# A two-layer Mamba, attention and expert kernel: transposed state sums, convolution on TensorE, wide attention products, and GpSimd's state group scanned in place in SBUF

## What is computed

```python
# layer 0, Mamba
xz = x @ W_in;  x_main, z = split(xz)
x_conv = silu(causal_depthwise_conv(x_main, conv_w, conv_b))     # 4 taps
ssm = x_conv @ W_x                                               # 1 + 16 + 16 columns
delta = softplus(ssm[..., 0:1] * dt_w + dt_b)
A = -exp(A_log)
dA = exp(delta[..., None] * A)
dBx = (delta * x_conv)[..., None] * B_in[:, :, None, :]
# for each time step:  h = dA_t * h + dBx_t ;  y_t = sum over n of h[., n] * C_t[n]
y = (y + D * x_conv) * silu(z)
return y @ W_out
# layer 1, attention, for each of 4 batches and 8 heads
scores = (q + pe) @ (k + pe).T / sqrt(128), causal
attn = softmax(scores) @ v ;  out = attn (all heads side by side) @ Wo.T
```

## Time and profile before

| what | us |
|---|---|
| median of 3 runs (3016.66 to 3021.09) | 3020.17 |
| the profiled execution | 3014.69 |
| its span, first to last instruction | 3013.0 |
| VectorE busy in the span | 2185.5 (73%) |
| TensorE busy in the span | 2631.4 (87%) |
| GpSimd busy in the span | 1233.8 (41%) |
| ScalarE busy in the span | 1230.1 (41%) |

### The profile page before, as it was taken

One profiled execution on the slowest core, in us unless ns is written; L12 is line 12 of the kernel. 1 busy time (PEld: TensorE's weight loads), 2 busy tenths in 40 slices (PEclk: granted clock), 3 DMA queues, 4 the chain that ended last, 5 costly groups with the idle time before them and its releaser, 6 DMA issues. The chain is left out here.

```text
span 3013.0 us, 39940 instructions
## 1 busy us (share of the span) xinstructions
PE 2631.4 (87%) x12440; PEld 1810.1 (60%) x12441; DVE 2185.5 (73%) x4715; ACT 1230.1 (41%) x2272; POOL 1233.8 (41%) x518
## 2 busy tenths in 40 slices
PE   6788888888887759999599999999999999839998
PEld 3233333333433559999377767776777677727776
DVE  4999999999999646666476667766776667525554
ACT  4566566566564215554133324332432243201111
POOL 1698998998999125666000000020002000224444
PEclk8899999999999659999799999999999999959999
DMA  4545555555556253333300000000000000125554
GB/s 154 174 148 179 171 162 172 180 160 178 166 167 189 96 166 59 63 63 58 130 29 1 1 1 29 1 30 16 1 1 29 15 1 1 43 90 127 126 126 72
DMA packets 150095, 269.26 MB, mean 89 GB/s; under 512 B 18300, under 2 KB 106412, under 8 KB 149292
## 3 DMA queue, kind: packets, MB, share of 16 engines
q1 hardware_dynamic: 120972, 227.12, 23.6%
q0 software_dynamic: 28416, 38.05, 7.6%
q10 hardware_dynamic: 544, 2.10, 0.2%
HBM read 209.65 MB, written 57.56 MB: 89 GB/s over the span
## 5 line engine op out<-in xcount | busy, mean ns | idle before, releaser
L692 POOL TENSOR_TENSOR dbx<-u,b_all 128x2048 f32<-128x2048 f32 x128 | 577.6, 4527 | 104.3 <-DVE u L766 49.5
L1677 POOL DMA_INDIRECT slots<-at_r_rows,slot_of x64 | 63.7, 995 | 1171.8 <-DVE slot_of L2022 1153.5
L432 PE MATMUL y_ps<-hc,ident 128*128 128x512 f32 x768 | 403.6, 643 | 117.5 <-DVE hc L846 116.3
L585 ACT ACTIVATE da_ps<-delta,a_neg 128x512 f32<-128x512 f32 x512 | 346.4, 689 | 323.6 <-DVE hc L846 316.7
L1888 ACT COPY at_pt<-at_pt_ps 128x512 f32<-128x512 f32 (+3 forms) x384 | 171.5, 481 | 511.8 <-PE at_pt_ps L1778 510.7
L432 PEld LDWEIGHTS y_ps<-hc,ident 128*128 128x128 f32 x768 | 139.0, 198 | 343.9 <-DVE hc L846 246.5
L1790 PE MATMUL at_o_ps<-at_pt,at_v 128*128 128x128 f32 x2304 | 300.0, 276 | 1.9 <-DVE at_attn L2096 1.9
L1767 PE MATMUL at_s_ps<-at_qk 128*128 128x512 f32 (+3 forms) x768 | 291.4, 489 | 5.0 <-DVE at_v L2072 3.1
L1790 PEld LDWEIGHTS at_o_ps<-at_pt,at_v 128*128 128x128 f32 x2304 | 278.0, 192 | 9.7 <-issue 9.7
L1878 ACT ACTIVATE at_probs<-at_s_ps,at_small 128x128 f32<-128x128 f32 (+7 forms) x256 | 191.8, 749 | 207.9 <-DVE at_small L2083 207.5
L846 DVE TENSOR_TENSOR hc<-da_ps,c_all 128x512 f32<-128x512 f32 x384 | 256.7, 669 | 0.1
(11 more groups left out here) (315 smaller groups left out, 4891.7 us busy)
## 6 DMA issues: line engine op xcount, KB each, us to landing
b_all<-bc_rows SPq DMA_DIRECT2D x128, 512.0 KB, 4.5
c_all<-bc_rows SPq DMA_DIRECT2D x128, 512.0 KB, 4.7
e_w<-L_ffn_w SPq DMA_DIRECT2D x32, 512.0 KB, 5.5
slots<-zeros SPq DMA_DIRECT2D x40, 260.0 KB, 6.3
e_xs<-slots SPq DMA_DIRECT2D x16, 650.0 KB, 7.2
w<-L_ffn_W SPq DMA_DIRECT2D x24, 384.0 KB, 8.9
more<-zeros SPq DMA_DIRECT2D x16, 256.0 KB, 4.5
sums<-x SPq DMA_DIRECT2D x8, 512.0 KB, 7.0
```

The costliest lines, as they stand in the source:

```text
L432: mm = nc.tensor.matmul(y_ps[par][:], sh.ident[:], hc[:, at % RING_H, :], start=False, stop=last)
L585: nc.scalar.activation(da_ps[s % RING_DA][:], delta[:, c % 2, m, :], ACT.Exp, scale=sh.a_neg[:, m, n:n + 1]).then_inc(S["da_ready"], 1)
L692: nc.gpsimd.tensor_tensor(dbx[:, at % RING_DBX], pair, rows, ALU.mult).then_inc(S["dbx_ready"], 1)
```

## The change

Mamba:

- The sum over the states is formed transposed. `sum_states` takes 128x128 slices of `hc` or `own_h` as the stationary side and the identity as the moving one, four PE transposes that accumulate in `y_ps`. After a half, `turn_back` (4 transposes for each channel block) and ScalarE's `take_back` turn y back into `u`.
- For chunks 1 to 7 the convolution leaves VectorE: `convolve` on TensorE adds three matmuls with diagonal tap matrices to the bank, ScalarE's `take_conv` copies the bank to `x_conv`. GpSimd builds the 12 tap matrices at the start (`taps`, in the idle `sh.mods`).
- `delta_product` becomes one matmul that broadcasts row 0 of `bc_sb`; the 128-column copies of w_x go.
- `keep_state` goes to ScalarE, ahead of the decay that takes over the bank.
- The decay of an own step is written to its slot of `own_h` (SBUF), and VectorE's scan reads and writes that slot. The `da_ps` ring then holds other steps alone. ScalarE, no longer VectorE, waits until TensorE has summed the slot's previous content.
- New step numbers in the hand-written order; `gate_y` behind products 8 and 13, `finish_delta` and `multiply_u` both behind product 14 and ahead of product 15.

Attention:

- `weigh` takes half a head (512 query columns) at once: 4 matmuls of 512, 384, 256 and 128 columns, then 8 of 512 (five times), 384, 256 and 128, spread over the following tiles. `keep` copies 128x512, twice per head.
- Two of the eight output tiles are ahead of the last half head's `weigh`.
- `mods2` and its 1 MB load are gone; the rows are loaded per batch into `sh.mods` behind the use of the old ones. `more` shares memory with `attn`; the output of a batch is stored in the loop.

The diff, cut to its core:

```diff
@@ phase_mamba
-        PE_OUT, PE_Z, PE_MAIN, PE_DELTA, PE_BC, PE_NEXT, PE_TURN = (3, 6), (0, 1), (5, 8, 13, 16), 31, 32, (34, 40), (46, 47, 51, 54)
-        ACT_Y, ACT_OUT, ACT_Z, ACT_MAIN, ACT_SILU = 2, (13, 18), (8, 9), (18, 20, 24, 29), 33
-        ACT_RAW, ACT_SOFT, ACT_BC, ACT_NEXT, ACT_XN, ACT_TURN = (36, 38, 41, 44), 46, 42, (52, 53), (51, 53, 55, 59), (62, 63)
-        DVE_OUT, DVE_CONV, DVE_RSTD, ACT_KEEP = (33, 62), (17, 18, 27, 29), 40, 5
-        POOL_W, POOL_GATE, POOL_DELTA, POOL_U, POOL_OWN = 1, 2, 13, 15, 2
+        PE_OUT, PE_Z, PE_MAIN, PE_DELTA, PE_BC, PE_NEXT, PE_TURN = (30, 31), (0, 1), (1, 2, 10, 15), 31, 31, (36, 39), (49, 51, 53, 54)
+        PE_BACK, PE_CONV, ACT_CONV, ACT_BACK = (18, 25, 34, 35), (2, 6, 17, 18), (13, 16, 27, 30), (30, 31, 46, 48)
+        ACT_Y, ACT_OUT, ACT_Z, ACT_MAIN, ACT_SILU = 6, (36, 41), (8, 9), (10, 12, 19, 26), 35
+        ACT_RAW, ACT_SOFT, ACT_BC, ACT_NEXT, ACT_XN, ACT_TURN = (43, 44, 46, 47), 49, 42, (50, 56), (48, 52, 54, 60), (61, 62)
+        DVE_OUT, DVE_RSTD, ACT_KEEP = (36, 41), 36, 6
+        POOL_W, POOL_GATE, POOL_DELTA, POOL_U, POOL_OWN = 6, (8, 13), 14, 14, 2
@@ TensorE
+            def convolve(c, m):
+                pe.wait_ge(S["main_copied"], c * MD + m + 1)
...
+                for j in range(DC - 1):
+                    mm = nc.tensor.matmul(proj_ps[m % 2][:], taps[:, m, j, :], x_main[:, m % 2, j:j + CH], start=False, stop=(j == DC - 2),
+                                          skip_group_check=True)
+                mm.then_inc(S["conv_summed"], 1)
+            def turn_back(c, m):
+                bank_free(c, f"back{m}")
+                pe.wait_ge(S["y_taken"], c * MD + m + 1)
...
+                    mm = nc.tensor.transpose(bank[:, j * P:(j + 1) * P], u[:, c % 2, m, j * P:(j + 1) * P], sh.ident[:])
@@ delta_product
-                    mm = nc.tensor.matmul(proj_ps[1][:], sh.w_delta[:, k, :], x_conv[:, c % 2, k, :],
-                                          start=(k == 0), stop=(k == MD - 1))
+                pe.wait_ge(S["bc_copied"], c + 1)
+                nc.tensor.matmul(proj_ps[1][:], one[:], bc_sb[0:1, :], start=True, stop=True).then_inc(S["delta_done"], 1)
@@ sum_states
-                    mm = nc.tensor.matmul(y_ps[par][:], sh.ident[:], hc[:, at % RING_H, :], start=False, stop=last)
+                for j in range(CT):
+                    at = slice(j * P, (j + 1) * P)
+                    mm = nc.tensor.matmul(y_ps[par][:, at], source[:, at], sh.ident[:], start=False, stop=(last and j == CT - 1), is_transpose=True)
@@ decay (ScalarE)
-                nc.scalar.activation(da_ps[s % RING_DA][:], delta[:, c % 2, m, :], ACT.Exp,
-                                     scale=sh.a_neg[:, m, n:n + 1]).then_inc(S["da_ready"], 1)
+                if is_own(s):
...
+                    elif before >= 0:
+                        act.wait_ge(S["own_summed"], before * GS + i + 1)
+                    out = own_h[:, i // 2, i % 2, :]
+                else:
...
+                    out = da_ps[v % RING_DA][:]
+                    if v >= RING_DA:
+                        act.wait_ge(S["hc_ready"], v - RING_DA + 1)
+                        bc, bs = step_of(v - RING_DA)
+                        if bc % CPB == 0:
+                            nc.scalar.copy(state[:, bs:bs + 1], da_ps[v % RING_DA][:, CH - 1:CH]).then_inc(S["states_kept"], 1)
+                            act.wait_ge(S["states_kept"], hc_at(bc // CPB, bs) + 1)
+                nc.scalar.activation(out, delta[:, c % 2, m, :], ACT.Exp, scale=sh.a_neg[:, m, n:n + 1]).then_inc(S["da_ready"], 1)
@@ scan (VectorE)
-                h = da_ps[s % RING_DA][:]
-                out = h
...
-                    out = own_h[:, i // 2, par, :]
-                nc.vector.tensor_tensor_scan(out, h, dbx[:, at % RING_DBX, i // 2, par, :], 0.0 if c % CPB == 0 else state[:, s:s + 1],
+                h = own_h[:, i // 2, par, :] if is_own(s) else da_ps[hc_at(c, s) % RING_DA][:]
+                nc.vector.tensor_tensor_scan(h, h, dbx[:, at % RING_DBX, i // 2, par, :], 0.0 if c % CPB == 0 else state[:, s:s + 1],
                                              ALU.mult, ALU.add).then_inc(S["scanned"], 1)
@@ phase_attention
-            sp.dma_start(mods2[:], d["mod_rows"][1, 3:5].partition_broadcast(P)).then_inc(S["route_in"], 16)
+            def load_route_mods(rb):
+                sp.wait_ge(S["row_ready"], (rb + 1) * TPB)
...
+                sp.dma_start(sh.mods[:, 0:2, rb, :], d["mod_rows"][1, 3:5, rb].partition_broadcast(P)).then_inc(S["route_in"], 16)
@@ weigh
-                    for j in range(i + 1):
-                        last = nc.tensor.matmul(o_ps[:], v[:, h % 2, j, :], pt[:, n % 2, j, :], start=(j == 0), stop=(j == i))
+                    first = max(j - half * CT, 0) * P
+                    last = nc.tensor.matmul(o_ps[:, first:], v[:, h % 2, j, :], pt[half][:, j, first:], start=(j == 0), stop=(j == (half + 1) * CT - 1))
```

More of the change, by code:

```diff
@@ L160, in phase_mamba @@
         h_in = sb("h_in", [P, 2, KE, CH])
-        bc_sb = sb("bc_sb", [P, CH])
+        bc_sb, one = sb("bc_sb", [1 + 2 * NS, CH]), sb("one", [1, P])
         b_all = sb("b_all", [P, RING_B, 2, CH])
@@ L417, in sum_states @@
                 par = i % 2
-                if k % HS < 2:
-                    halves = c * HALVES + hf
-                    if halves:
-                        pe.wait_ge(S["y_taken"], (halves - 1) * 2 + par + 1)
-                    nc.tensor.matmul(y_ps[par][:], d_diag[:, hf * 2 + par, :], x_conv[:, c % 2, hf * 2 + par, :], start=True, stop=False)
-                last = k % HS >= HS - 2
+                first, last = k % HS < 2, k % HS >= HS - 2
+                halves = c * HALVES + hf
+                if first and halves:
+                    pe.wait_ge(S["y_taken"], (halves - 1) * 2 + par + 1)
+                if first:
+                    for j in range(CT):
+                        at = slice(j * P, (j + 1) * P)
+                        nc.tensor.matmul(y_ps[par][:, at], x_conv[:, c % 2, hf * 2 + par, at], d_diag[:, hf * 2 + par, :], start=(j == 0), stop=False)
                 if g in OWN:
@@ L426, in sum_states @@
                         pe.wait_ge(S["own_ready"], own_to(c, hf, g))
-                    mm = nc.tensor.matmul(y_ps[par][:], sh.ident[:], own_h[:, i // 2, par, :], start=False, stop=last)
-                    mm.then_inc(S["own_summed"], 1)
+                    source, done = own_h[:, i // 2, par, :], S["own_summed"]
                 else:
@@ L673, in _ @@
                 take_y(CHUNKS - 1, m)
+            for m in (2, 3):
+                take_back(CHUNKS - 1, m)
             for pair in range(2):
@@ L729, in _ @@
             nc.gpsimd.memset(sh.zeros[:], 0.0).then_inc(S["zeros_set"], 1)
+            nc.gpsimd.memset(one[:], 1.0).then_inc(S["one_set"], 1)
+            pool.wait_ge(S["ident_set"], 2)
+            pool.wait_ge(small_in, 48)
+            for m in range(MD):
+                for j in range(DC - 1):
+                    nc.gpsimd.tensor_scalar(taps[:, m, j, :], sh.ident[:], sh.conv_w[:, m, j:j + 1], None, ALU.mult).then_inc(S["taps_set"], 1)
             for c in range(CHUNKS):
@@ L1564, in phase_attention @@
     PIECES = 3 * CPB
+    EARLY_OUT = 2
     with ExitStack() as ctx:
@@ L1577, in phase_attention @@
         probs = sb("probs", [P, 3, T])
-        pt = sb("pt", [P, 2, TPB, P])
+        pt = [sb(f"pt{half}", [P, CT * (half + 1), CH]) for half in range(2)]
         attn = sb("attn", [P, HEADS, T])
@@ L1641, in _ @@
                 sp.wait_ge(S["summed"], b * TPB)
[L1642 removed]
+                if b > 1:
+                    sp.wait_ge(S["out_done"], (b - 1) * TPB)
+                sp.dma_start(more, d["more0"][b * T:(b + 1) * T, :].rearrange("(j p) e -> p j e", p=P)).then_inc(S["x_in"], 16)
                 sp.wait_ge(S["x_in"], b * 32)
[L1644 to L1647 removed]
+                load_route_mods(b - 1)
+                if b > 1:
+                    store_out(b - 2)
+            load_route_mods(B - 1)
+            store_out(B - 2)
+            store_out(B - 1)
             sp.wait_ge(S["x_stored"], 16 * B)
@@ L1804, in batch @@
                     project(0, i)
-                for n in range(N + 3):
+                for n in range(N + 2):
                     if n < N:
```

300 lines of the change are left out of this document (174 added, 126 removed).

## The result

| | before | after |
|---|---|---|
| median us (range, runs) | 3018.62 (3016.66 to 3021.09, 4) | 3113.82 (3112.89 to 3115.66, 4) |
| ratio, 95% interval | | 1.0316 [1.0298, 1.0334] |
| span of the profiled execution | 3013.0 | 3112.2 |
| Mamba loop, start of the first to start of the last scan | 913.8 | 1026.8 |
| span outside it | 2099.2 | 2085.4 |

The change makes the kernel slower by 95 us (3113.8 us measured); the forecast was 3118 us, slower. In the profiled executions the loop takes 113 us more and all else 14 us less.

What follows compares the result with a forecast made beforehand. VectorE was taken to bound the Mamba loop and TensorE attention. From the profiled 3014.7 us, plus 109 in the loop, minus 11 in attention, came 3113, and 5.5 to the median gave 3118 us; range 3068 to 3172 us.

Steps and rivals of the forecast that it cites:

- The deciding term: Mamba loop: own scans with two SBUF operands and GpSimd instructions reading SBUF block each other; loop 109 us longer.
- group 13: Last own scans of a chunk, meeting finish_delta, multiply_u and product 15 in a row: 12.6 us later, 4 in the last chunk.
- Waits elsewhere: Mamba loop: stray waits, like those on ScalarE spread over the loop before, allowed 8 us.
- The rest of Mamba hides: Mamba: ScalarE's added copies (88 of 128 us a chunk) and TensorE's new work (71 us) stay covered; small terms cancel.
- the cover named for it: ScalarE in the Mamba loop: own decays no longer take ring slots, which should hide its added state copies.
- The 5.5 us: Whole kernel: the profiled execution was 5.5 us below the median, so this was added, 3113 to 3118 us.
- Attention: Attention phase: wider weigh passes save 8 us and an earlier w_o load 3; sum 11 us less.
- The start: Start of attention: TensorE waits for w_o; 1 MB less loaded ahead is worth 0 to 4.2 us, 3 taken.
- The signs named in advance: Profile after: own scans mean 2.7 us, GpSimd busy about 82%, TensorE below 75%, no VectorE convolution or state copy, weigh 7.8.
- No exclusion: Mamba loop: scans don't exclude GpSimd, 107 us a chunk, loop 853 us, kernel 2946 us; chance 0.12.
- Exclusion without blocks: Mamba loop: chunk is only GpSimd's work plus own scans, 123.7 us; loop 989 us, kernel 3082 us; chance 0.10.
- TensorE at its lower clock: Mamba loop: transposes with gaps run at half clock and bind, 143 us a chunk; kernel 3183 us; chance 0.08.

Runs made afterwards that it cites:

- e1: Kernel after, with own decays back in the PSUM ring and own scans reading them there; all else of the change stays; 2991.29 us, ratio to before 0.9909.
- e5: Kernel after, with own decays and scan outputs in different SBUF slots of a five-slot buffer, so nothing is in place; ratio to before 1.0346.
- e6: Kernel after, with GpSimd's 128 products replaced by memsets of the same size that read nothing; one run, no ratio, loop 892.3 us.
- e9: Kernel after, with only the fourth step of each own group having its decay in SBUF, the other three in PSUM; ratio to before 0.9972.
- e7: Kernel before, with only the attention phase of the kernel after; ratio to before 0.9951.
- e8: e1 with three numbers of ScalarE's list moved earlier (taking y, the SiLU block, the copy of B and C); ratio to before 0.9836.
- e10: e8 with a seventh slot in the ring hc; 2963.71 us, ratio to before 0.9819.
- e4: Kernel after, with multiply_u moved behind product 15 and the last own output in GpSimd's list; 3101.47 us, ratio to before 1.0276.
- e2: Kernel before, with only own decays written to own_h and scanned in place; old order, convolution and sums stay; 3182.82 us.

## Why the prediction was right

**The deciding term.** "I take exclusion": shown. e1 takes the decay out of SBUF and wins 123 us, e5 keeps it there without the scan in place and wins nothing, e6 has no exclusion beside a memset that doesn't read, and in e9 scans with a PSUM operand pass beside a product. The Trainium skill's rule ("SBUF — State Buffer", section "Who interferes with whom") holds for the scan too, which the page doesn't name: 5.24 us for 1.2 beside one product.

**Its size was too high, by 26 us.** Walked: 4.0, 4.0, 4.0 and 12.6 us a chunk and 4 for the last group 13, 188 us; measured 4.0, 4.1, 3.3 and 9.6 us (3.9 for the last group 13), 162. The term that was mis-sized is group 13, 21 of the 26 us. I had GpSimd's row of three instructions wholly ahead of its scans. In the trace `finish_delta` has run for 2.6 us (435.59 to 438.22) when the first own scan comes, so that much of the row is over. Group 9 loses less, probably as its first scan, step 36, is late anyway behind ScalarE's SiLU block: in chunk 0, where that wait is longest (4.4 us), it loses nothing.

**Waits elsewhere were too low, by 28 us.** I allowed 8 us for the loop; it is 36. "The rest of Mamba hides" doesn't hold in two places. ScalarE: the cover named for it exists, since without it (e1) idle time rises to 72 us, but it doesn't reach step 36, where VectorE waits 2.5 to 4.4 us in chunks 0 to 6 and 0.7 in chunk 7, 21 us in all. TensorE: I said that `hc` lets VectorE go on for 20 us against some 14 needed. I counted the wait for `bc_sb` and not the output product that now stands at steps 30 and 31 beside it:

```profile
527.76 0.60 PE L475 MATMUL y_ps<-ident,hc 128*128 128x128 f32 x4
528.20 1.89 PE L485 MATMUL proj_ps<-w_out,u 128*128 128x256 f32 x8
...
535.12 1.89 PE L485 MATMUL proj_ps<-w_out,u 128*128 128x256 f32 x8
537.37 3.62 PE L443 MATMUL proj_ps<-x_conv,w_x 128*33 128x512 f32 x8
542.36 1.09 PE L452 MATMUL proj_ps<-bc_sb,one 1*128 1x512 f32 x2 [1.37 <-ACT bc_sb L616]
```

From 528.20 to 543.38 us there is one state sum (0.44 us), 15 us without the others, and VectorE waits 14.7 us for TensorE in the whole loop.

So the loop, forecast 109 us longer and measured 113, is close to it partly by luck: two errors of opposite sign, 26 and 28 us, cancel. The range, 3068 to 3172 us, had room for either. The 5.5 us that the sum adds for the distance of the profiled execution from the median had no counterpart: after, the profiled execution took 3114.1 us (3113 forecast), and the median is 3113.8.

**Attention.** Forecast 11 us less; e7 gives 15 (11 to 19), the profiles 13.8 outside the loop. `weigh` gives 11.4 of busy time (300.0 to 288.6), where I took 8 in a range of 5 to 10. The start gives 2.5: the wait ahead of the first transpose falls from 32.22 to 29.67 us, with 3 taken. The attention phase as a whole, first to last instruction, falls from 1202.8 to 1185.9 us; some 3 us come back ahead of the loop, which starts 1.5 us later and not 2 earlier, and behind attention.

```profile
1573.65 0.66 PE L1790 MATMUL at_qk_ps<-ident,at_rows 128*128 128x128 f32 x2 [29.67 <-DVE at_rows L2146]
```

**The signs named in advance.** Own scans: mean 2.5 us (2.7 said), maximum 5.57. GpSimd busy 837.4 of 1031 us, 81% (82 said). TensorE 67%, below 75. No convolution and no state copy on VectorE. All as said. For `weigh` the view has busy time, in which neighbours overlap, 9.0 us a head for 9.4, and not the pitches from which 7.8 for 8.0 was worked out.

**The rivals.** *No exclusion*, priced at 2946 us, is not this kernel. But e1, e8 and e10 show what its price missed: at 107 us a chunk it let VectorE and GpSimd run on unhindered, and measured is 113 in e1 and 110 in e10, as ScalarE then sets the pace in places. *Exclusion without blocks*, 3082 us, falls: a chunk takes 129 us and not 123.7, though ScalarE's and TensorE's waits are part of that, and e4, with the same work in another order, gains 12 us, which a sum can't. *TensorE at its lower clock* (its terms add up to 3185 us, not 3183) doesn't bind. The granted clock in the loop does fall, from 0.95 to 0.79 at 67% busy. In e1, with the same transposes, it is 0.84 at 73%, and in e2, which keeps the old sums, 0.88 at 74%:

```profile
79.00:985.00 906.00, 665.29 (x3193) 475.92 (x3194) 833.29 (x937) 609.42 (x1092) 819.04 (x191) 0.84 0.55 171
```

```profile
79.00:1160.00 1081.00, 804.30 (x1748) 334.28 (x1749) 1057.61 (x1205) 543.57 (x838) 843.58 (x191) 0.88 0.45 142
```

Part of the fall in after is a result of the exclusion. While VectorE goes through group 13 of chunk 1, TensorE gets no `hc` and stands 11.48 us, up to 326.85. In that stretch, at 319.1, the clock falls to the lower of its two levels (0.50) and stays there up to 336.2; TensorE then has hardly anything but the sums:

```profile
326.85 1.11 PE L475 MATMUL y_ps<-ident,hc 128*128 128x128 f32 x4 [11.48 <-DVE hc L921]
...
319.10:336.20 17.10, 8.21 (x35) 7.01 (x36) 17.10 (x16) 5.63 (x9) 14.76 (x4) 0.50 0.29 85
```

What the transposes themselves have to do with it was not separated: they stand behind idle time there, and TensorE's busy time differs between the kernels too. TensorE doesn't set the loop, since it still stands 23.8 us for `hc` in a chunk of after (470 to 600 us). The rule that transposes don't count for the clock (the Trainium skill, "TensorE: Matmul & The Clock Gate", Part 4) is neither shown nor refuted by these runs.

## What to carry to other kernels

Before an operand is moved from PSUM to SBUF, look at what else that VectorE instruction reads and what GpSimd does meanwhile: if both its tensor inputs are then in SBUF and GpSimd's instruction reads SBUF, it costs the rest of that GpSimd instruction, here 4.0 us on top of a scan of 1.2, in place or not. If it can't be avoided, put such an instruction where GpSimd's is nearly over or waits, and don't put several GpSimd instructions in a row beside it. And a list that another engine no longer holds up shows the next one: after such an edit the waits move to whichever engine was ordered for the old pace, and a loop that agrees with the forecast may do so because errors cancel, so compare the terms and not only the sum.

## What the runs showed of the hardware

- The exclusion holds for the scan with two SBUF operands: 5.24 us for 1.2 beside a GpSimd product of 4.53. It is the same with the output in place or in another slot of SBUF (2483 ns on average in after, 2478 in e5), and it doesn't arise beside a GpSimd memset (1.26 us in e6). An output in PSUM with both inputs in SBUF was not tried.
- It works both ways, and where neither engine waits for anything else they alternate instruction by instruction: GpSimd's 4.5 us become 5.3 to 5.4, and three scans last 11.38 us.
- A GpSimd memset of 128x2048 takes 1.81 us, where a product of that size takes 4.53.
- The same kernel, before, takes 3017 to 3019 us beside e1 to e4 and e10 and 3056 to 3057 beside e5 to e9. The record has e1 to e4 and e7 to e9 on the same chip, so the chip by itself isn't shown to be the cause. The loop is the same; in the traces the difference lies in attention, where the same code lasts 1224 to 1227 us in e5 to e9 and 1186 in after, e1, e4 and e10. The cause stays open.
